# Layer norms and key spreading on VectorE in a windowed-attention and mixture-of-experts block, one core

## What is computed

```
x = x + conv(ln_c(x))          # windowed attention: 7x7 windows, 12 heads of 8 channels, shift of 3/4, relative bias, masks
t = tokens(x)
t = t + ffn(ln_t(t))           # 4 experts 96 -> 384 -> 96 with exact gelu, top 2 of 4 gates, softmax gate weights

ln(v):   m = mean(v, -1);  s = var(v, -1);  (v - m) / sqrt(s + eps)
conv:    qkv = xw @ w_qkv.T + b_qkv;  p = softmax(q k^T / sqrt(8) + bias + mask);  (p v) @ w_proj.T + b_proj
ffn:     out = sum over experts of gate_e * (gelu(x @ w1_e + b1_e) @ w2_e + b2_e)
```

## Time and profile before

| | |
|---|---|
| three runs, median (lowest to highest) | 7466.94 us (7466.27 to 7467.78) |
| span of the profiled execution | 7472.1 us |
| PE busy | 7129.8 us, 95% |
| PEld busy | 5658.9 us, 76% |
| DVE busy | 5951.8 us, 80%, 17441 instructions |
| ACT busy | 4441.6 us, 59% |
| POOL busy | 2691.2 us, 36% |
| PE clock granted | 0.9 or more of full in every fortieth of the span |

### The profile page before, as it was taken

The page is one execution under the profiler, slowest core; times in us unless marked ns, Lnnn a source line. Parts: engine busy times, 40 slices in busy tenths (PEclk is TensorE's granted clock), DMA queues, the critical chain, the costliest instruction groups (busy, mean ns, idle before and its releaser), DMA issues.

```text
span 7472.1 us, 236413 instructions
## 1 busy us (share of the span) xinstructions
PE 7129.8 (95%) x87040; PEld 5658.9 (76%) x87040; DVE 5951.8 (80%) x17441; ACT 4441.6 (59%) x8959; POOL 2691.2 (36%) x1799
## 2 busy tenths in 40 slices
PE   5999999999999999999999999999999999999998
PEld 4777777777777777777777777777777777777777
DVE  6788778888788887878787788787888778887886
ACT  4566655665566655656565566655665566655664
POOL 3333333333333333333333333333333333333332
PEclk9999999999999999999999999999999999999999
DMA  1111111111111111111111111111111111111110
GB/s 49 35 32 35 33 34 32 34 34 34 32 34 35 33 33 34 34 33 34 33 34 33 34 32 34 33 34 32 35 33 34 32 34 35 34 32 34 34 33 18
DMA packets 168131, 250.97 MB, mean 34 GB/s; under 512 B 44272, under 2 KB 129008, under 8 KB 166768
## 3 DMA queue, kind: packets, MB, share of 16 engines
q1 hardware_dynamic: 166896, 234.60, 11.0%
HBM read 80.28 MB, written 38.54 MB: 16 GB/s over the span
## 4 chain that ended last, share of the span: by engine, by line
PE 52%; issue 27%; POOL 13%; DVE 4%; ACT 2%; SPq 1%; POOLq 0%; DMA 0%; DVEq 0%
PE ps_f L1010 18%; PE ps_t L926 10%; PE ps_o L945 7%; PE ps_s L916 4%; POOL rstd L399 4%; POOL rstd L383 3%; PE ps_f L954 3%; PE ps_f L1007 3%; PE ps_s L907 3%; ACT pt_sb L498 2%; POOL xn L393 2%; POOL xn L388 2%; POOL p_sb L417 2%; PE ps_f L865 1%; DVE stat L691 1%
## 5 line engine op out<-in xcount | busy, mean ns | idle before, releaser
L417 POOL TENSOR_TENSOR p_sb<-p_sb,s_rec 113x588 f32<-113x588 f32 x1024 | 1213.6, 1185 | 3244.9 <-DVE s_rec L677 3244.9
L1010 PE MATMUL ps_f<-w_sb,g_sb 128*112 128x96 f32 x18432 | 1963.7, 261 | 0.0
L1010 PEld LDWEIGHTS ps_f<-w_sb,g_sb 128*112 128x112 f32 x18432 | 1916.3, 178 | 0.0
L483 ACT ACTIVATE g_sb<-ps_f 128x392 f32<-128x392 f32 x3072 | 1524.3, 497 | 287.8 <-PE ps_f L859 217.7
L494 ACT ACTIVATE p_sb<-s_sub 113x588 f32<-113x588 f32 x1024 | 723.3, 706 | 1612.2 <-DVE s_sub L665 1612.2
L857 PE MATMUL ps_f<-x_hi,w_hi 128*128 128x392 f16 x3072 | 1040.7, 339 | 117.7 <-issue 103.5
L663 DVE TENSOR_REDUCE s_max<-ps_s 113x12 f32<-113x588 f32 x1024 | 770.8, 753 | 412.1 <-PE ps_s L916 405.6
L858 PE MATMUL ps_f<-x_lo,w_hi 128*128 128x392 f16 x3072 | 1038.3, 338 | 0.0
L859 PE MATMUL ps_f<-x_hi,w_lo 128*128 128x392 f16 x3072 | 1036.9, 338 | 0.0
L675 DVE TENSOR_REDUCE s_sum<-p_sb 113x12 f32<-113x588 f32 x1024 | 779.5, 761 | 199.7 <-ACT p_sb L494 161.9
L926 PE MATMUL ps_t<-ident,p_sb 113*113 113x113 f32 x6144 | 854.3, 275 | 49.9 <-POOL p_sb L417 49.9
(11 more groups left out here) (114 smaller groups left out, 10867.8 us busy)
## 6 DMA issues: line engine op xcount, KB each, us to landing
k_st<-qk_hi SPq DMA_DIRECT2D x768, 49.0 KB, 2.0
q_st<-qk_hi SPq DMA_DIRECT2D x768, 49.0 KB, 2.0
xr<-x SPq DMA_DIRECT2D x224, 139.1 KB
out<-xr SPq DMA_DIRECT2D x224, 139.1 KB
xa<-x SPq DMA_DIRECT2D x224, 136.5 KB
k_st<-qk_lo SPq DMA_DIRECT2D x384, 49.0 KB, 2.0
q_st<-qk_lo SPq DMA_DIRECT2D x384, 49.0 KB, 2.0
xa<-x SPq DMA_DIRECT2D x224, 10.5 KB
```

The source lines that it names most:

```text
L417: nc.gpsimd.tensor_tensor(p, p, s_rec[:, :].unsqueeze(2).broadcast_to([SPAN, HEADS, WW]), ALU.mult).then_inc(pnorm_done, 1)
L483: nc.scalar.activation(g_sb[:, chunk, half * STRIP:(half + 1) * STRIP], h_bank[k % 3][:, 0:STRIP], ACT.Gelu, scale=1.0 / WSCALE).then_inc( ...
L1010: ins = T.matmul(y[:, k * C:(k + 1) * C], g_sb[:, e * CPE + c, j * LANES:(j + 1) * LANES], w2_sb[:, e * CPE + c, :], start=False, stop=(c ...
```

## The change

- `spread_keys`: four tensor_scalar operations a unit instead of twelve; each takes all three groups of k_st for one head.
- second norm: `centre` is gone, and `scale` is one tensor_scalar per tile, (x - mean) * rstd, seven in a unit. PE's `transpose2` waits per tile instead of per part.
- `ln1_stats`: moved from the tail of a step to the head of the next one, for the same unit, behind `spread_keys` and ahead of `router_b`.

```diff
--- before.py
+++ after.py
@@ -118,7 +118,7 @@
 N_XHI, N_X1LO = 4, 4
 N_COMB = 7 * EXPERTS
 N_STACK = 16 * 3 * GROUPS
-N_KBD = GROUPS * GH
+N_KBD = GH
 QSCALE = HD ** -0.5
 QK_SCALE = (QSCALE / WSCALE, 1.0 / WSCALE)
 
@@ -242,7 +242,7 @@
         sum_done, rec_done, pnorm_done = sem("sum_done"), sem("rec_done"), sem("pnorm_done")
         res_done = sem("res_done")
         stat2_done, aggr2_done, var2_done = sem("stat2_done"), sem("aggr2_done"), sem("var2_done")
-        rstd2_done, centre2_done = sem("rstd2_done"), sem("centre2_done")
+        rstd2_done = sem("rstd2_done")
         norm2_done, x2lo_done = sem("norm2_done"), sem("x2lo_done")
         gate_ready = sem("gate_ready")
         router = sem("router")
@@ -652,10 +652,9 @@
             def spread_keys(a):
 
                 dve.wait_ge(k_in, at(a, N_STACK, N_STACK))
-                for g in range(GROUPS):
-                    for j in range(GH):
-                        V.tensor_scalar(k_bd[0:C, g, j, :], k_st[:, g, :], head_rows[:, j:j + 1], None,
-                                        ALU.mult).then_inc(kbd_done, 1)
+                for j in range(GH):
+                    V.tensor_scalar(k_bd[0:C, :, j, :], k_st[:, :, :], head_rows[:, j:j + 1], None,
+                                    ALU.mult).then_inc(kbd_done, 1)
 
             def softmax_pair(a, n):
                 scores = ps_s[0:SPAN, 0:HEADS * NB].rearrange("p (h k) -> p h k", k=NB)[:, :, 0:WW]
@@ -700,27 +699,19 @@
                     V.tensor_scalar(ve2[:, j0:j0 + n], mv2[:, j0:j0 + n, 1], EPS_T, None, ALU.add
                                     ).then_inc(var2_done, 1)
 
-                def centre(k, j0, n):
-                    V.tensor_tensor(xn2[:, j0:j0 + n, :], rows[:, j0:j0 + n, :],
-                                    mv2[:, j0:j0 + n, 0:1].broadcast_to([LANES, n, C]), ALU.subtract
-                                    ).then_inc(centre2_done, 1)
-
                 def scale(k, j0, n):
-                    dve.wait_ge(centre2_done, at(f, 2, k + 1))
                     dve.wait_ge(rstd2_done, at(f, 2, k + 1))
-                    V.tensor_tensor(xn2[:, j0:j0 + n, :], xn2[:, j0:j0 + n, :],
-                                    rstd2[:, j0:j0 + n].unsqueeze(2).broadcast_to([LANES, n, C]),
-                                    ALU.mult).then_inc(norm2_done, 1)
+                    for t in range(j0, j0 + n):
+                        V.tensor_scalar(xn2[:, t, :], rows[:, t, :], mv2[:, t, 0:1], rstd2[:, t:t + 1],
+                                        ALU.subtract, ALU.mult).then_inc(norm2_done, 1)
 
                 dve.wait_ge(xr_in[u], f[0] * per + (f[1] // UPI + 1) * per)
                 first_part, second_part = (0, 0, 4), (1, 4, 3)
                 sums_of(*first_part)
                 variances(*first_part)
                 sums_of(*second_part)
-                centre(*first_part)
                 variances(*second_part)
                 scale(*first_part)
-                centre(*second_part)
                 scale(*second_part)
                 x2_low(f, 0)
                 x2_low(f, 1)
@@ -822,9 +813,6 @@
                 if b is not None:
                     qk_low(b, 0)
                     qk_low(b, 1)
-                    c = following(b)
-                    if c is not None:
-                        ln1_stats(c)
                     qk_low(b, 2)
                 residual(a)
                 if b is not None:
@@ -837,6 +825,8 @@
             def step(f, a, b, u):
                 if a is not None:
                     spread_keys(a)
+                    if b is not None:
+                        ln1_stats(b)
                 router_b(f)
                 if a is not None:
                     softmax_pair(a, 0)
@@ -960,8 +950,8 @@
                 for k, (j0, n) in enumerate(((0, 4), (4, 3))):
                     if k == 1 and b is not None:
                         qk(b, 3)
-                    pe.wait_ge(norm2_done, at(f, 2, k + 1))
                     for j in range(n):
+                        pe.wait_ge(norm2_done, at(f, W, j0 + j + 1))
                         ins = T.transpose(bank[5 + k][0:C, j * LANES:(j + 1) * LANES], xn2[:, j0 + j, :],
                                           ident[0:LANES, 0:LANES])
                     ins.then_inc(t2_done, 1)
```

## The result

The changed kernel takes **7741.64 us**, median of four runs (7739.57 to 7744.53), against 7466.68 for the kernel before (7466.27 to 7467.78). The ratio is 1.0367, with a 95% interval of 1.0353 to 1.0381: 3.7% slower, or 275 us. The profiled execution has a span of 7742.0 us against 7472.1, a difference of 269.9. The forecast was 7712.

A forecast was written before the change was run, and what follows sets the result against it. PE (95% busy) was taken as the bound, with 0.76 us of DVE slack at the head; keys, statistics and held router make the softmax 2.55 us late in 96 steps, tail 0: 7467 + 245 = 7712 us, range 7455 to 7780.

The forecast's parts named there:

- The keys' rate: DVE's merged keys at the head: two elements a slot, 1.36 us each, 5.4 us for four against 4.18.
- the fast one: Rival, keys at the head keep four elements a slot, 3.0 us for four: 7453 to 7481, middle 7467; chance 0.28.
- Statistics and router: Head of step: statistics add 1.95 us, POOL's L388 and L393 hold the router's L776 and L780; softmax 2.55 us late.
- T: Router's start on DVE at the head, after keys of 5.4 and statistics of 1.95 us: 3750.7, against 3747.53 before.
- The order-by-luck rival: Router at the head: L776 gets in ahead of L388, only L780 held; 1.3 us late, 7592; chance 0.25 at half rate.
- had nothing been held: Router at the head: POOL's pow as slow as its median, nothing held, 0.55 us late: 7520.
- The tail: Second norm at the step's end, up to PE's hidden products: 0, between -0.11 and +0.5 us a step.
- Holding of POOL's second L399: Second norm at the tail: DVE's back-to-back operations may hold POOL's L399, so the later three tiles may not come sooner.
- The clock: Rival: PE's clock falls after standing 2.3 us before scores(1), up to 2.9 us more a step, 7990; 0.07, shared with slower keys.
- The turns: Loop turns, 30 times: gates end at 1046.95, before the softmax at 1048.00 that waits for PE, so nothing is lost.
- The sum: Whole kernel: 96 regular steps x 2.55 = 245 us, added to the median 7467: 7712 us, 3.3% slower.
- Idle at the tail: Tail, once the statistics have left it: DVE waits 2.7 us for PE's projection.

The follow-up runs named there:

- one_run_keys: The changed kernel with k_bd laid out head before group, so each merged key operation writes one run of 2352 elements; 7471.40 us, ratio 1.0000.
- norm1_between: The changed kernel with POOL's three first-norm operations behind its first three scalings of the probabilities instead of at the head; 7522.67 us, ratio 1.0072.
- keys_only: The kernel before with only the keys merged into four operations of 2352 elements, three rows out; 7489.56 us, ratio 1.0023.
- undo_keys: The changed kernel with twelve keys operations again, statistics at the head and one-operation second norm kept; 7547.23 us, ratio 1.0104.
- norm2_one_run_keys: The kernel before with the one-operation second norm and four key operations writing one run each, first-norm statistics left at the tail; 7456.63 us, ratio 0.9982.

## Why the prediction was right

**The keys' rate: right.** Two elements a slot was taken between rates for which no row stood, with 1.36 us for the pitch of one operation; it is 1.35 (5.39 / 4). One_run_keys shows that it is the shape of the output and nothing else. No row of the kernel before showed the rate, and with the fast one the forecast would have been 7467.

**Statistics and router: right, with its mechanism.** Predicted were T at 5.4 + 1.95, pow 0.15 behind T, L776 held by L388 and L780 by L393, and gates at T + 4.6. Measured: 5.39 + 1.96, 0.15, the same two held (lines L767 and L771 now), T + 4.40. The lateness is 2.43 against 2.55, and PE stands 2.56 us in all where 2.9 was forecast. The estimate of 0.2 us for the router in pow's way is the term that was too large: L388 starts at T + 1.59, not T + 1.8, since pow took its undisturbed 1.48. The order-by-luck rival occurred in none of the 126 steps with a first norm. Norm1_between came close to its price, had nothing been held (7523 measured, 7520 forecast), but by another order of POOL and with the late sum in it, which the price didn't have.

**The tail: the term was mis-sized.** I put it at 0 and said it could at best win 0.11, the gap of PE before its transposes. It wins 0.14. The step that failed is "what follows is PE's transposes, ACT's copy, then x_lo": in both traces L732 or L723 follows DVE's own last scaling by less than 0.1 us, and PE's hidden product follows it. DVE bounds this stretch in the steps read, so what counts is the length of DVE's chain from the residual's addition (5.57 us to x_lo before, 5.42 now), and not PE's idle rows. The seven operations take 1.92 us, not 1.3 to 1.75, yet their first starts sooner since the centring is gone (3.41 us behind the addition of the residual, 3.76 before). Holding of POOL's second L399 didn't come: it takes 0.91 where it took 1.10.

**The clock: a rival that came true in part.** I gave it 0.07 as a case of its own that would hit every step with up to 2.9 us. It hit little more than one regular step in three, with about 0.9 us each (59.46 against 58.57), some 26 us in the span with the late sum of L674, which nobody had foreseen. The failure is the form of it: it isn't a different outcome, but a term on top of the forecast once PE stands for 2 us. It came in the turns too, which the prediction left as they were.

**The turns: the wait was right, the sum was not.** 0 was forecast, and DVE does still wait 0.61 us there. The steps of this position grew by 13.8 us in all, 9.7 of them in the 30 turns, and the longer stretches of lower clock account for these (12 x 1.27 = 15, less 4 at the tail). The term was put at nothing because PE's wait covers DVE; that PE's clock behind the turn could stay down longer was not in it.

**The sum.** Forecast: 96 x 2.55 = 245. Measured: 96 x (2.43 - 0.14) = 220, the clock and the late sum 26, the turns 14, and the remaining 10 in regular steps that grow by up to 0.2 more than 2.29. Two errors made the forecast too high (0.12 us a step at the head, 0.14 at the tail, 25 us together) and two too low (40 us). The direction and the cause are shown by the runs; that the figure came within 30 us is partly luck.

**Idle at the tail: right.** 2.7 us for the projection were forecast. DVE waits 0.58 us for ACT in front of the third L648 and 2.03 for PE: 2.61.

In the expectations for the experiments, keys_only, one_run_keys and norm1_between came out 12 to 22 us above what was expected. In keys_only POOL's operations moved with the edit and met others, which I hadn't reckoned with. In the other two the largest part found is the late sum in one step of four.

## What to carry to other kernels

Fewer instructions are only cheaper if the engine keeps its rate: before operations are merged, look at how the input and the output fall into runs after merging, and put the destination in an order that keeps both alike. Work that is moved to where an engine has slack takes its followers with it; here the statistics took POOL's two wide operations along, so that these kept running beside a chain of tiny ones and stretched two of those from 0.2 to 1 us. They had done so before the change, within the slack; once the slack is spent, the same hold costs 1.85 us a step. Look first for the stretch where the engine itself is the late one: of the three edits only the one made there won anything, and it is worth keeping alone. And where the clock at each turn of a loop changes by itself, read a difference of 10 us step by step before explaining it.

## What was not expected of the hardware

- PE's clock fell behind only some of stands that look alike: leaving out the last one, in 35 of 94 regular steps after 2.10 us in the changed kernel, 31 of them at one position in the image, in 64 of 94 after 2.28 to 2.37 us, and in none after 0.81 to 0.91.
- At the stands of over 3 us on issue the lower level lasts 3.4 us at some turns and 6.8 at others: 13 and 17 turns in the kernel before, 1 and 29 in the changed one, 24 and 6 in undo_keys.
- The row of a float32 memset is shorter than what the memset costs: 1.64 us for 1900 elements, with 0.46 us of idle in front that the view puts down to DVE's own gates, against 2.01 us between its neighbours.
- In three kernels (the change, one_run_keys, norm1_between) DVE starts one operation 0.35 us late in the same one of four steps each time: 0.47 us behind the exponential that it reads, in the others 0.12.
- A tensor_scalar of 112x96 float32 with two columns as operands lasts 323 ns, and seven in a row follow each other at 0.267 us (1.92 less 0.32, over six). That is above both ends of the prediction's bracket for the pitch (0.19 to 0.25).
- POOL's exponential L407 took 5.62 us beside the twelve keys operations and 4.78 in the changed kernel, where it ends at 3765.20. It is not the rate of the keys: beside four operations at the full rate (norm2_one_run_keys) it takes 4.79, and with twelve again (undo_keys) 5.62. In these traces it goes with their number.
